# Layer 0's product: six blocks in the first pass over the matrix, with a maximum of their own

## The chip, the cores and the metric

The kernel runs on one core of one Trainium2 chip. The metric is the device time of one execution in microseconds (us); smaller is better. A core has TensorE (PE; it multiplies matrices and writes PSUM, a memory of eight banks of 512 fp32 columns in 128 partitions), VectorE (DVE), ScalarE (ACT), GpSimd (POOL), and SyncE (SP), which here only issues transfers (DMAs). Each engine takes its instructions in order; they wait for one another by semaphores (`wait_ge`, `then_inc`).

## What is computed

A graph network of four layers over N = 2708 nodes with D = 128 features. All share one adjacency matrix `adj` (2708 x 2708 fp32, 29 MB, some nine entries a row, all positive in these inputs). Layers 0 and 1, which the change touches:

```python
# layer 0
hw = x @ W
h_plus, h_minus = (adj > 0) @ hw, (adj < 0) @ hw
e_plus  = leaky_relu(h_plus @ a1 + h_minus @ a2, 0.2)      # one score per node
e_minus = leaky_relu(h_minus @ a1 + h_plus @ a2, 0.2)
scores  = where(adj > 0, e_plus[None, :], where(adj < 0, e_minus[None, :], -9e15))
x = layernorm(x + softmax(scores, axis=1) * adj @ hw)
# layer 1
A = adj + eye;  d = A.sum(1) ** -0.5
x = layernorm(x + relu(d[:, None] * A * d[None, :] @ (x @ W1.T + b1)))
# layers 2 and 3: attention with four heads, then messages with gelu,
# both over the non-zero entries; layernorm after each
```

Without negative entries each column of the softmax is a weight `exp(e_plus[j] - max)`. Layer 0 is then a product of `adj` with hw scaled per node, divided by the sums of the weights over each row's non-zero entries.

## The kernel before

**Tiling.** The 2708 nodes are 22 blocks of 128 rows, the last (block 21) of 20. A block of `adj` or its transpose is 1354 KB. `ring` holds nine blocks of the transpose, `rows` two blocks of `adj` itself. The output columns are six chunks (five of 512, one of 148), one PSUM bank each (banks 0 to 5). SP issues the ring's loads, POOL most of the rows' loads.

**First pass** (0 to 122 us). Every transposed block is loaded (`load_ring`, L841), ScalarE turns it into its signs in bf16 (`binT`, L1019), and TensorE adds `signs x u` for all nodes in 22 products of four columns (L122, `ps<-u,binT`); u = hw @ a1 lies in `u3`. The last block gives the scores (`zd`, L1574), their maximum goes through TensorE to all partitions (`nmx0`, L1587), ScalarE makes the weights (L1025).

**Extraction.** VectorE takes from every block of `adj` the eight largest entries and their places in each of six segments of 452 columns (`extract_segment`, L1532 and L1522), then the rest for that block (`extract_rest`), which also gives the row sum for layer 1 (`dinv`). A block is seven pieces. `FIRST` = 5 blocks are extracted in the first pass, up to `AHEAD` = 15 during layer 0's product, 18 pieces in the transition, the rest after it. POOL loads a rows buffer again when its block is extracted (`v_row`, L962), and does a lookup per block. Later layers need the edges found this way.

**Layer 0's product** (to 212, then in a transition to 303). Blocks go backwards, 21 to 0: the last nine are still in the ring. ScalarE scales hw by the weights (L1032) and makes the signs again (L1039). TensorE does six chunks of the share (`share0`, fp32, `ps<-ring,hwu`) and six of the sums of weights (`weight_sums`, bf16, banks 6 and 7). The last `TAIL` = 7 blocks are done chunk by chunk (`tail0`), so that a finished chunk can be transposed, normalised and projected for layer 1 while the next is computed (the loop over `SLOTS`, L1092 and L1313).

**Layer 1** (303 to 360). Nine blocks, 0 to 8, are in the ring; blocks 0 to 7 are multiplied within the transition (`shares1_until`), block 8 on in a loop, the last `TAIL1` = 5 by chunks (`tail1`). hw1 of blocks below `AHEAD` is scaled by 1/sqrt(row sum) as it is made (`projected1`). For the others `scaled_late` (L1082) does square root and scaling when ScalarE comes to block `LATE` = 14 of its own loop: 22 passes that look for negative entries (L1117). TensorE waits for that at block 15. VectorE waits for the square root in `row_scales`, with nothing of the extraction left behind it. After its loop ScalarE copies finished chunks from PSUM (L1053). VectorE waits for the end of ScalarE's loop (`c_neg`) ahead of `after_layer1`.

**Layers 2 and 3** (to 786) gather rows from tables in HBM with indirect DMAs from POOL (L939). `near0` is such a table; only the path for other inputs reads it.

## Time and profile before

| | |
|---|---|
| median of three runs | 786.44 us (783.33 to 786.92) |
| the profiled execution | 787.66 us |
| its span, first to last instruction | 785.9 us |
| PE busy / DVE / ACT / POOL | 445.2 / 480.0 / 301.0 / 333.8 us |
| DMA moved | 117.20 MB, mean 149 GB/s |
| mean granted TensorE clock | 0.747 |

A row of the view by stages gives the stretch, its length, the busy time of PE, of its weight loads (PEld), DVE, ACT and POOL, each with its count of instructions, the granted clock, the DMA share and GB/s.
### The profile page before, as it was taken

Reading aid. Unit: us, or ns where it says so; the run is one execution under the profiler, and the core shown is the slowest. Engines: PE = TensorE matmul, PEld = TensorE weight load, DVE = VectorE, ACT = ScalarE, POOL = GpSimd, SP = SyncE. Lnnn points to the kernel's source line nnn. Section 1 sums busy time; section 2 is a strip of 40 time slices with the busy share of each in tenths; the row PEclk is TensorE's granted clock in tenths of the full one; section 3 lists DMA queues with packets and bytes.
Section 4 is the critical chain, followed back from the end, with each engine's and each line's share of the span. In section 5 each row is a group of like instructions: output and inputs, shape, how many; then the busy total and the mean of one; then the engine's idle time right before and its main releaser. Section 6 shows DMA issues by size and latency. Waiting matters only on the chain.

```text
span 785.9 us, 6700 instructions
## 1 busy us (share of the span) xinstructions
PE 445.2 (57%) x1987; PEld 269.0 (34%) x1987; DVE 480.0 (61%) x1457; ACT 301.0 (38%) x363; POOL 333.8 (42%) x492
## 2 busy tenths in 40 slices
PE   4221118999999999999843855304504404405231
PEld 4121113444455655444632734203303303303120
DVE  2419608988946569523454559539849749748564
ACT  3565364458823316995611302203213213213131
POOL 7204502555522126400055356726636736736700
PEclk9555555999999999999865886656757757757655
DMA  8999992999712124990022211211112112111200
GB/s 317 367 424 420 398 324 110 365 398 387 298 71 72 56 72 156 425 374 1 28 73 56 73 44 43 54 30 51 47 37 50 52 32 51 50 33 50 54 8 13
DMA packets 32697, 117.20 MB, mean 149 GB/s; under 512 B 8518, under 2 KB 19636, under 8 KB 23892
## 3 DMA queue, kind: packets, MB, share of 16 engines
q1 hardware_dynamic: 19970, 78.21, 25.3%
q0 software_dynamic: 9952, 38.49, 15.5%
q10 hardware_dynamic: 2734, 0.01, 0.2%
q8 instruction: 17, 0.28, 0.1%
q14 instruction: 24, 0.20, 0.1%
HBM read 111.15 MB, written 5.55 MB: 148 GB/s over the span
## 4 chain that ended last, share of the span: by engine, by line
PE 40%; DVE 25%; DMA 11%; issue 10%; another core or an unknown queue 8%; ACT 3%; SPq 1%; ACTq 0%; DVEq 0%
PE ps L122 38%; DMA ring<-in_adjT_dram 11%; DVE agg L1858 4%; DVE G L1855 3%; DVE G L1843 2%; DVE A L1747 1%; DVE st L1761 1%; DVE M L1725 1%; SPq L842 1%; DVE Mh L1724 1%; DVE t L1779 1%; DVE t L1782 1%; DVE t L1781 1%; DVE yo L1788 1%
## 5 line engine op out<-in xcount | busy, mean ns | idle before, releaser
L939 POOL DMA_INDIRECT G<-near,IX x147 | 140.3, 954 | 44.8 <-issue 44.8
L122 PE MATMUL ps<-ident,agg 128*128 128x128 f32 (+1 forms) x44 | 14.3, 420 | 192.6 <-DVE agg L1858 160.2
L122 PE MATMUL ps<-ring,hwu 128*128 128x512 f32 (+3 forms) x264 | 114.3, 586 | 1.0 <-ACT hwu L1032 1.0
L122 PE MATMUL ps<-ring,xT_s 128*128 128x512 f32 (+1 forms) x264 | 108.0, 553 | 0.0
L1522 DVE FIND_INDEX8 I<-V,rows 128x8 uint32<-128x452 f32 (+1 forms) x132 | 82.1, 627 | 0.0
L939 POOL DMA_INDIRECT Go<-near,IO x44 | 43.6, 990 | 89.7 <-DVE IO L1741 59.5
L1532 DVE MAX8 V<-rows 128x8 f32<-128x452 f32 (+1 forms) x132 | 79.9, 618 | 0.8
L122 PEld LDWEIGHTS ps<-ident,agg 128*128 128x128 f32 (+1 forms) x44 | 9.4, 260 | 198.2 <-DVE agg L1858 162.6
L122 PEld LDWEIGHTS ps<-ring,hwu 128*128 128x128 f32 (+1 forms) x264 | 51.0, 203 | 63.9 <-issue 62.7
L1019 ACT ACTIVATE binT<-ring 128x2708 bf16<-128x2708 f32 (+1 forms) x22 | 53.9, 2459 | 45.2 <-DMA ring<-in_adjT_dram 45.2
L1039 ACT ACTIVATE binT<-ring 128x2708 bf16<-128x2708 f32 (+1 forms) x22 | 53.9, 2456 | 29.5 <-PE ps L122 29.5
L962 POOL DMA_DIRECT2D rows<-in_adj_dram x18 | 10.9, 606 | 125.7 <-DVE I L1522 125.7
L122 PE MATMUL ps<-u,binT 128*128 128x4 bf16 (+1 forms) x484 | 18.1, 167 | 80.5 <-ACT binT L1019 80.5
L122 PE MATMUL ps<-E,M 128*128 128x273 f32 (+2 forms) x192 | 53.9, 440 | 16.1 <-DVE IO L1741 8.7
L122 PEld LDWEIGHTS ps<-ring,xT_s 128*128 128x128 f32 x264 | 45.5, 192 | 43.7 <-issue 43.1
L1117 ACT ACTIVATE binT<-ring 128x2708 bf16<-128x2708 f32 (+1 forms) x22 | 53.8, 2444 | 0.0
L939 POOL DMA_INDIRECT G<-near2f,WIX x22 | 21.6, 983 | 75.6 <-DMA near2f<-hwu 69.2
L122 PEld LDWEIGHTS ps<-E,M 128*128 128x128 f32 x192 | 40.2, 232 | 29.2 <-issue 22.1
L122 PEld LDWEIGHTS ps<-u,binT 128*128 128x128 bf16 (+1 forms) x484 | 16.0, 103 | 82.7 <-ACT binT L1019 79.6
L1188 ACT ACTIVATE std<-mv,eps 128x2 f32<-128x2 f32 x22 | 6.5, 296 | 95.6 <-remote 44.2
L969 POOL TENSOR_TENSOR look<-places,posf 128x336 f32<-128x336 f32 (+1 forms) x22 | 16.4, 744 | 56.4 <-DVE posf L1551 56.4
L1858 DVE TENSOR_REDUCE agg<-G 128x128 f32<-128x1024 f32 x21 | 39.5, 1881 | 0.7
(258 smaller groups left out, 843.9 us busy)
## 6 DMA issues: line engine op xcount, KB each, us to landing
ring<-in_adjT_dram SPq DMA_DIRECT2D x46, 1354.0 KB, 15.5
rows<-in_adj_dram POOLq DMA_DIRECT2D x17, 1354.0 KB, 9.5
rows<-in_adj_dram SPq DMA_DIRECT2D x4, 1354.0 KB, 23.7
G<-near,IX POOLq DMA_INDIRECT x147
xT_s<-in_xT_dram SPq DMA_DIRECT2D x1, 1354.0 KB, 6.3
near<-hwu SPq DMA_DIRECT2D x1, 1344.0 KB
out_dram<-yo SPq DMA_DIRECT2D x21, 64.0 KB
near2f<-hwu SPq DMA_DIRECT2D x5, 256.0 KB
```

Of the source, the lines that this page charges most:

```text
L122: return pe.matmul(dst, lhsT, rhs, start=start, stop=stop, skip_group_check=True)
L939: pool.indirect_dma_start(out=dst, out_offset=None, in_=table, in_offset=bass.IndirectOffsetOnAxis(ap=index, axis=0), engine_sem=o_g).then ...
L962: pool.dma_start(rows[0:rn(n + ROWS), n % ROWS, :], adj[(n + ROWS) * P:(n + ROWS) * P + rn(n + ROWS), :]).then_inc(s_later[n % ROWS], 16)
L969: lk.done(pool.tensor_tensor(look[0:r, :, :], places[0:r, :].unsqueeze(1).broadcast_to([r, TOP, SEGS * 8]), posf[0:r, n, :].unsqueeze(2).b ...
L1019: act.activation(binT[0:rn(j), j % 2, :], ring[0:rn(j), j % RING, :], ACT.Sign).then_inc(c_sg, 1)
L1039: act.activation(binT[0:rn(j), p % 2, :], ring[0:rn(j), j % RING, :], ACT.Sign).then_inc(c_sg, 1)
L1117: act.activation(binT[0:rn(j), j % 2, :], ring[0:rn(j), j % RING, :], ACT.Relu, scale=-1.0, accum_out=negs[0:rn(j), j:j + 1]).then_inc(c_n ...
L1522: return dve.max_index(I64[0:rn(n), n % 2, 8 * s:8 * s + 8], V64[0:rn(n), n % 2, 8 * s:8 * s + 8], segment(n, s))
L1532: dve.max(V64[0:rn(n), n % 2, 8 * s:8 * s + 8], segment(n, s)).then_inc(v_max, 1)
L1843: dve.tensor_tensor(G3[0:r, q, 0:TOP, :], G3[0:r, q, 0:TOP, :], own.unsqueeze(1).broadcast_to([r, TOP, D]), ALU.add).then_inc(v_pre, 1)
L1855: few.done(dve.tensor_tensor(at, at, slot_weights[0:r, n, :].unsqueeze(2).broadcast_to([r, TOP + 1, D]), ALU.mult))
L1858: dve.tensor_reduce(agg[0:r, n % 2, :], at.rearrange("p k d -> p d k"), AX.X, ALU.add).then_inc(v_agg, 1)
```

## The change

Six blocks of layer 0's product, 9 to 14 (`TAKEN`), are done in the first pass. Their scores are needed early, so xT is first multiplied by a replicated column `wa_all`, which leaves u of all nodes in every partition of banks 0 to 5, and VectorE computes the six blocks' scores from their rows of `adj` (`zdA`), the maximum of these six, and the weights against that maximum. Four of the six blocks of rows lie in ring slots until they are extracted (`HELD`), two in `rows`; they are loaded first, and extracted first (`EXTRACT`). The transposed blocks are loaded as 9 to 14, 2 to 8, 15 to 21, 0, 1 (`STREAM`); the sixth to ninth of them each wait for an extraction to free a slot, the tenth to fifteenth for a share of TensorE. When the global maximum is known, ScalarE multiplies banks 0 to 5 in place, and VectorE banks 6 and 7, by `fall` = exp(own maximum - global maximum), and 16 blocks follow (`LAYER0`: 15 to 21, 0, 1, 2 to 8). The row sums by signs move to bank 5. near0 is stored after the last load. `AHEAD` is 14, and the late scaling has two batches: extractions 14 to 16 (blocks 8, 15, 16), square root at ScalarE's block 4, needed at TensorE's block 8; and 17 to 21, at 14, needed at 17. The product that folds the attention vector of layer 2 moves from the pass to the transition. The gathers no longer count a semaphore of their issue. The diff, cut to its core:

```diff
-EARLY = 4
-FIRST = 5
-AHEAD = 15
-LATE = 14
+GROUP = 6
+HELD = GROUP - ROWS
+FIRST = 8
+AHEAD = 14
+LATE = [(14, 4), (17, 14)]
...
+        by_rows, maxima, folded = bank(5, 152, 4 * NB), bank(5, 256, P + 4), bank(7, 32, 9)
...
+        TAKEN = list(range(RING, RING + GROUP))
+        AGAIN = list(range(2 * RING + GROUP - NB, RING))
+        KEPT = list(range(RING + GROUP, NB)) + list(range(2 * RING + GROUP - NB))
+        STREAM = TAKEN + AGAIN + KEPT
+        LAYER0 = KEPT + AGAIN
+        REST = len(LAYER0)
...
+        FIRST1 = HELD + NB + len(AGAIN) - RING
+
+        def slot(q):
+            return (q - FIRST1) % RING
+
+        def landed(q):
+
+            return 16 * (q // RING + 1)
...
+        def at_pass(i):
+            return HELD + i
+
+        def at_layer0(p):
+            return HELD + NB - RING + p
+
+        def at_layer1(j):
+            return FIRST1 + j
+
+
+        EXTRACT = TAKEN + [n for n in range(NB) if n not in TAKEN]
...
+        BATCHES = [0, AHEAD] + [first for first, _ in LATE[1:]] + [NB]
...
+            for t in range(GROUP):
+                n = EXTRACT[t]
+                if t < HELD:
+                    load_ring(t, n, adj)
+                else:
+                    sp.dma_start(rows[:, (t - HELD) % ROWS, :], adj[n * P:n * P + P, :]).then_inc(s_rows[(t - HELD) % ROWS], 16)
+            for i in range(NB):
+                past = at_pass(i) - RING
+                if 0 <= past < HELD:
+                    sp.wait_ge(v_row, past + 1)
+                elif past >= HELD:
+                    sp.wait_ge(c_sg, past - HELD + 1)
+                    if past - HELD < GROUP:
+                        sp.wait_ge(p_l0, past - HELD + 1)
+                load_ring(at_pass(i), STREAM[i])
+            sp.wait_ge(c_hw, 8)
...
+            for p in range(len(AGAIN)):
+                sp.wait_ge(p_l0, GROUP + p + 1)
                 sp.wait_ge(c_sg, NB + p + 1)
-                load_ring(NB - RING - 1 - p)
+                load_ring(at_layer0(RING + p), AGAIN[p])
...
-                                        in_offset=bass.IndirectOffsetOnAxis(ap=index, axis=0), engine_sem=o_g).then_inc(signal, 16)
-
-
-            for dst, src in [(w2c[:, 0:D], w2), (w2T_s, w2T), (w1T_s[:, :], w1T), (w3c[:, 0:D], wdT),
+                                        in_offset=bass.IndirectOffsetOnAxis(ap=index, axis=0)).then_inc(signal, 16)
...
+                if HELD <= t < NB - ROWS:
+                    to, b = EXTRACT[t + ROWS], (t - HELD) % ROWS
+                    if t + ROWS == FIRST:
+                        pool.wait_ge(c_sg, NB - 2)
+                    pool.wait_ge(v_row, t + 1)
+                    pool.dma_start(rows[0:rn(to), b, :], adj[to * P:to * P + rn(to), :]).then_inc(s_later[b], 16)
+                pool.wait_ge(v_pos, t + 1)
...
+            for i, j in enumerate(STREAM):
+                if i == 2:
+                    act.wait_ge(v_e, 3)
+                    act.activation(wts[:, 0, TAKEN[0]:TAKEN[0] + GROUP], eeA[:, :], ACT.Exp, bias=nm1[:, 0:1]).then_inc(c_w, 1)
+                    act.wait_ge(c_w, 1)
+                    for k, n in enumerate(TAKEN):
+                        act.activation(hws[:, k, :], hwu[:, n, 0:D], ACT.Copy, scale=wts[:, 0, n:n + 1]).then_inc(c_hws, 1)
+                act.wait_ge(s_ring[slot(at_pass(i))], landed(at_pass(i)))
+                if i >= 2:
+                    act.wait_ge(p_e, i - 1)
+                    if i - 2 < GROUP:
+                        act.wait_ge(p_z, i - 1)
+                act.activation(binT[0:rn(j), i % 2, :], of_ring(at_pass(i), rn(j)), ACT.Sign).then_inc(c_sg, 1)
...
+            act.activation(fall[:, :], nm1[:, :], ACT.Exp, bias=nmx0[:, 0:1], scale=-1.0).then_inc(c_w, 1)
+            act.wait_ge(c_w, 3)
...
+            for at, m in chunks:
+                act.activation(ps[:, at:at + m], ps[:, at:at + m], ACT.Copy, scale=fall[:, 0:1]).then_inc(c_w, 1)
...
+            def scaled_late(k):
+                first, last = BATCHES[k + 1:k + 3]
+                act.wait_ge(v_rs, 2 * k + 3)
+                act.activation(dinv[:, 0, first:last], dinv[:, 0, first:last], ACT.Sqrt, bias=ones[:, 0:1]).then_inc(c_dinv, 1)
+                act.wait_ge(v_rs, 2 * k + 4)
                 act.wait_ge(c_hw1, CH)
-                for n in range(AHEAD, NB):
-                    last = act.activation(hw1[0:rn(n), n, :], hw1[0:rn(n), n, :], ACT.Copy, scale=dinv[0:rn(n), 1, n:n + 1])
-                last.then_inc(c_hw1, 1)
+                for t in range(first, last):
+                    n = EXTRACT[t]
+                    late = act.activation(hw1[0:rn(n), n, :], hw1[0:rn(n), n, :], ACT.Copy, scale=dinv[0:rn(n), 1, t:t + 1])
+                late.then_inc(c_hw1, 1)
...
+                for k, (_, at) in enumerate(LATE):
+                    if j == at:
+                        scaled_late(k)
...
+            for at, m in chunks:
+                last = mm(pe, ps[:, at:at + m], wa_all[:, :], xT_s[:, at:at + m], True, True)
+            last.then_inc(p_hw, 1)
...
+            def share_in_pass(i):
+                for at, m in chunks:
+                    last = mm(pe, ps[:, at:at + m], hws[:, i, :], of_ring(at_pass(i), P)[:, at:at + m],
+                              i == 0 and m == BANK, False)
+                last.then_inc(p_l0, 1)
+
+            for i, j in enumerate(STREAM):
+                pe.wait_ge(c_sg, i + 1)
+                for n in range(NB):
+                    last = mm(pe, by_rows[:, 4 * n:4 * n + 4][0:rn(n), :], binT[0:rn(j), i % 2, n * P:n * P + rn(n)], u3[0:rn(j), j, :],
+                              False, i == NB - 1)
+                last.then_inc(p_e if i < NB - 1 else p_ecol, 1)
+                if i < GROUP:
+                    if i == 0:
+                        pe.wait_ge(v_w3, 1)
+                    sums_of_weights(j, i % 2, i == 0)
+                    pe.wait_ge(c_hws, i + 1)
+                    share_in_pass(i)
...
+                    if p == 0:
+                        pe.wait_ge(c_w, 3 + c + 1)
+                    last = share0(p, c)
...
+                for k in range(len(LATE)):
+                    if j == min(EXTRACT[BATCHES[k + 1]:BATCHES[k + 2]]):
+                        pe.wait_ge(c_hw1, CH + k + 1)
...
+            dve.wait_ge(p_hw, 1)
+            for t in range(GROUP):
+                if t < HELD:
+                    dve.wait_ge(s_ring[slot(t)], landed(t))
+                    at = of_ring(t, P)
+                else:
+                    dve.wait_ge(s_rows[t - HELD], 16)
+                    at = rows[:, t - HELD, :]
+                few.done(dve.scalar_tensor_tensor(out=unused, in0=at, scalar=0.0, in1=ps[:, 0:N], op0=ALU.is_gt, op1=ALU.mult,
+                                                  accum_out=zdA[:, t:t + 1]))
+            few.done(dve.scalar_tensor_tensor(out=eeA[:, :], in0=zdA[:, :], scalar=SLOPE, in1=zdA[:, :], op0=ALU.mult, op1=ALU.max))
+            dve.tensor_reduce(emA[:, :], eeA[:, :], AX.X, ALU.max).then_inc(v_e, 1)
...
+            dve.wait_ge(c_w, 1)
+            weights_in_parts(slice(TAKEN[0], TAKEN[0] + GROUP))
...
+            dve.wait_ge(c_w, 3)
+            for to, b, m in ((slice(0, P), 6, BANK), (slice(0, 32), 7, BANK), (slice(32, 64), 7, chunks[5][1])):
+                dve.tensor_scalar(bank(b, 0, m)[to, :], bank(b, 0, m)[to, :], fall[to, 0:1], None, ALU.mult)
+            weights_in_parts(slice(0, NB))
...
+            done = at0 + 3 * CH
+            for k in range(1, len(BATCHES) - 1):
+                extract(done, BATCHES[k + 1] * BLOCK)
+                done = BATCHES[k + 1] * BLOCK
+                row_sums(k)
+                if k + 1 < len(BATCHES) - 1:
+                    extract(done, done + 2)
+                    done += 2
+                row_scales(k)
```

## Rows read from the trace of the kernel before

**Rows 1.** Stages: busy PE, PEld, DVE, ACT, POOL; clock, DMA share, GB/s

```profile
0.00:116.00 116.00, 27.90 (x513) 24.83 (x513) 47.32 (x183) 57.22 (x31) 39.16 (x94) 0.60 0.99 380
122.50:132.80 10.30, 10.24 (x18) 3.94 (x18) 9.99 (x37) 5.88 (x7) 1.59 (x3) 0.50 0.10 20
132.80:138.40 5.60, 5.60 (x8) 2.46 (x8) 5.60 (x17) 2.75 (x2) 3.73 (x9) 0.50 0.98 412
138.40:212.60 74.20, 74.20 (x288) 33.15 (x287) 65.24 (x235) 50.81 (x35) 42.60 (x88) 1.00 0.95 378
303.00:359.50 56.50, 56.50 (x169) 28.16 (x168) 25.88 (x95) 56.23 (x54) 16.35 (x38) 1.00 0.76 309
```

**Rows 2.** ScalarE, first pass: start, duration, line, operation, count, idle before

```profile
42.01 2.46 ACT L1019 ACTIVATE binT<-ring 128x2708 bf16<-128x2708 f32 x1 [4.04 <-DMA ring<-in_adjT_dram]
45.27 2.46 ACT L1019 ACTIVATE binT<-ring 128x2708 bf16<-128x2708 f32 x1 [0.80 <-DMA ring<-in_adjT_dram]
```

**Rows 3.** Start of one extraction, of the next, and the load freed between

```profile
123.16 0.28 DVE L1531 TENSOR_TENSOR rows<-rows,others 128x128 f32<-128x128 f32 x1
131.54 0.28 DVE L1531 TENSOR_TENSOR rows<-rows,others 128x128 f32<-128x128 f32 x1
130.64 0.60 POOL L962 DMA_DIRECT2D rows<-in_adj_dram  x1 [33.46 <-DVE I L1522]
```

**Rows 4.** End of the pass and start of layer 0, four engines

```profile
117.45 0.82 PE L122 MATMUL ps<-u,binT 20*128 20x4 bf16 x22 [1.52 <-ACT binT L1019]
118.31 0.23 DVE L1574 TENSOR_REDUCE zd<-ps 128x21 f32<-128x63 f32 x1 [26.62 <-PE ps L122]
121.76 0.31 ACT L1025 ACTIVATE wts<-ee,nmx 128x22 f32<-128x22 f32 x1 [4.36 <-DVE nmx L1587]
122.56 9.39 PE L122 MATMUL ps<-ring,hwu 20*128 20x512 f32 x12 [1.03 <-ACT hwu L1032]
```

**Rows 5.** Reads of PSUM by VectorE and ScalarE in the transition

```profile
234.32 1.13 DVE L1638 SCALAR_TENSOR_TENSOR tt<-ps,rz,X 128x128 f32<-128x128 f32 x4
218.93 0.60 ACT L1053 ACTIVATE accT<-ps 128x512 f32<-128x512 f32 x1 [1.42 <-PE ps L122]
```

**Rows 6.** Layer 0 blocks in the chain of waits; then TensorE at its tail

```profile
151.56 5.20 PE ps L122 x17
156.83 5.20 PE ps L122 x17
212.62 2.84 PE L122 MATMUL ps<-ring,hwu 128*128 128x512 f32 x6
```

**Rows 7.** Two microseconds of the first pass, columns as in Rows 1

```profile
18.00:19.00 1.00, 0.18 (x2) 0.06 (x1) 0.44 (x3) 1.00 (x3) 0.00 (x0) 1.00 1.30 201
22.00:23.00 1.00, 0.00 (x0) 0.00 (x0) 0.90 (x3) 1.00 (x1) 0.00 (x0) 0.81 1.28 298
```

**Rows 8.** ScalarE in layer 1, in order of time

```profile
303.13 2.44 ACT L1117 ACTIVATE binT<-ring 128x2708 bf16<-128x2708 f32 x1
337.35 0.28 ACT L1085 ACTIVATE dinv<-dinv,ones 128x7 f32<-128x7 f32 x1
337.90 2.16 ACT L1089 ACTIVATE xT_s<-xT_s,dinv 128x128 f32<-128x128 f32 x7 [0.27 <-DVE dinv L1606]
```

**Rows 9.** VectorE at the end of the extractions, in order of time

```profile
291.17 0.28 DVE L1531 TENSOR_TENSOR rows<-rows,others 128x128 f32<-128x128 f32 x1
324.55 0.17 DVE L1602 TENSOR_TENSOR dinv<-dinv,diag 128x7 f32<-128x7 f32 x1
337.66 0.20 DVE L1606 RECIPROCAL dinv<-dinv 128x7 f32<-128x7 f32 x1 [12.95 <-ACT dinv L1085]
```

**Rows 10.** TensorE in layer 1, in order of time

```profile
314.26 0.38 PE L122 MATMUL ps<-ident,xT_s 128*128 128x128 f32 x2
363.84 0.65 PE L1276 MATMUL ps<-ident,accT 128*128 128x128 f32 x4
```

**Rows 11.** A gather of layer 2 on POOL

```profile
400.83 0.96 POOL L939 DMA_INDIRECT G<-near2f,WIX  x1 [0.30 <-issue]
```

More of the change, by code:

```diff
@@ L839, in _, with load_ring @@
             sp.dma_start(xT_s[:, 0:N], xT).then_inc(s_x, 16)
-            def load_ring(j):
-                sp.dma_start(ring[0:rn(j), j % RING, :], adjT[j * P:j * P + rn(j), :]).then_inc(s_ring[j % RING], 16)
-            def load_rows(n):
-                if n >= ROWS:
-                    sp.wait_ge(v_row, n - ROWS + 1)
-                sp.dma_start(rows[0:rn(n), n % ROWS, :], adj[n * P:n * P + rn(n), :]).then_inc(s_rows[n % ROWS], 16)
-            for j in range(NB):
-                if j >= RING:
-                    sp.wait_ge(c_sg, j - RING + 1)
-                load_ring(j)
-                if j in (1, 4, 9, 13):
-                    load_rows((1, 4, 9, 13).index(j))
-                if j == NB - 8:
-                    sp.wait_ge(c_hw, 8)
-                    sp.dma_start(bass.AP(near0.tensor, 0, [[D, P], [P * D, NB - 1], [1, D]]), hwu[:, 0:NB - 1, 0:D]).then_inc(s_near, 16)
-                    sp.dma_start(near0[P * (NB - 1):N, :], hwu[0:LAST, NB - 1, 0:D]).then_inc(s_near, 16)
+            def load_ring(q, j, of=adjT):
+                sp.dma_start(of_ring(q, rn(j)), of[j * P:j * P + rn(j), :]).then_inc(s_ring[slot(q)], 16)
@@ L1239, in share0, with sums_of_weights @@
-            def share0(j, c):
-                at, m = chunks[c]
-                return mm(pe, ps[:, at:at + m], hwu[0:rn(j), j, 0:D], ring[0:rn(j), j % RING, at:at + m], j == NB - 1, j == 0)
-            def weight_sums(p):
-                j = NB - 1 - p
-                pe.wait_ge(c_sg, NB + p + 1)
+            pe.wait_ge(v_u3, 1)
+            for half in range(2):
+                mm(pe, bank(5, 256 * half, 256), zeros, w3[:, 0:8, :].rearrange("p n w -> p (n w)"), True, False)
+            def sums_of_weights(j, binary, first):
@@ new lines, in _, with share0, weight_sums @@
+            pe.wait_ge(v_e, 4)
+            mm(pe, maxima[0:2, 0:P], emx[:, :], ident[:, :], False, True).then_inc(p_gm, 1)
+            pe.wait_ge(v_e, 6)
+            mm(pe, maxima[:, P + 2:P + 4], ones[0:2, :], gm[0:2, 0:2], False, True).then_inc(p_gm, 1)
+            def share0(p, c):
+                at, m = chunks[c]
+                j = LAYER0[p]
+                return mm(pe, ps[:, at:at + m], hwu[0:rn(j), j, 0:D], of_ring(at_layer0(p), rn(j))[:, at:at + m], False, p == REST - 1)
+            def weight_sums(p):
+                pe.wait_ge(c_sg, NB + p + 1)
+                sums_of_weights(LAYER0[p], p % 2, False)
@@ L1265, in tail0 @@
             def tail0(c):
-                for j in range(TAIL - 1, -1, -1):
+                for p in range(MAIN0, REST):
                     if c == 0:
-                        pe.wait_ge(c_hws, NB - j)
-                        pe.wait_ge(s_ring[j % RING], in_layer0(j))
-                    last = share0(j, c)
+                        q = at_layer0(p)
+                        pe.wait_ge(c_hws, GROUP + p + 1)
+                        pe.wait_ge(s_ring[slot(q)], landed(q))
+                    last = share0(p, c)
                 last.then_inc(p_tail, 1)
@@ L1294, in share1 @@
                 at, m = chunks[c]
[L1295 removed]
+                last = mm(pe, ps[:, at:at + m], hw1[0:rn(j), j, :], of_ring(at_layer1(j), rn(j))[:, at:at + m], j == 0, False)
                 if j // 4 == c:
@@ new lines, in _, with lies, segment, places_of @@
+            dve.wait_ge(c_w, 1)
+            weights_in_parts(slice(TAKEN[0], TAKEN[0] + GROUP))
+            dve.wait_ge(k_set, 16)
+            def lies(t):
+                r = rn(EXTRACT[t])
+                return of_ring(t, r) if t < HELD else rows[0:r, (t - HELD) % ROWS, :]
+            def segment(t, s):
+                return lies(t)[:, s * SEG:min((s + 1) * SEG, N)]
+            def places_of(t, s):
+                r = rn(EXTRACT[t])
+                dve.wait_ge(v_max, t * SEGS + s + 1)
+                return dve.max_index(I64[0:r, t % 2, 8 * s:8 * s + 8], V64[0:r, t % 2, 8 * s:8 * s + 8], segment(t, s))
@@ L1608, in _, with row_scales @@
+            def row_scales(k):
+                b = slice(*BATCHES[k:k + 2])
+                dve.wait_ge(c_dinv, k + 1)
+                dve.reciprocal(dinv[:, 1, b], dinv[:, 0, b]).then_inc(v_rs, 1)
             dve.wait_ge(s_diag, 32)
-            dve.wait_ge(v_pos, AHEAD)
-            row_sums(slice(0, AHEAD))
+            row_sums(0)
             def stats(c):
```

260 lines of the change are left out of this document (116 added, 144 removed).

## The prediction

> **What bounds the kernel now.** I read the profile by stages first, then the order of time on each engine at the seams. [rows 1] show four regimes. Up to 116 us the transfers are the bound: DMA share 0.99 at 380 GB/s, TensorE busy 27.9 of 116 us. From 122.5 to 212.6 TensorE never stops: layer 0's product. The clock is 0.50 until 138.4 (1.2 GHz) and 1.00 (2.4 GHz) after that; before the rise it first worked on the block of 20 rows (122.5 to 132.8) and then 5.6 us on a full block. DMA stands at 0.95 to 0.98 there too, but TensorE waits for nothing. From 303 to 359.5 two engines are full at once, TensorE 56.5 and ScalarE 56.2 of 56.5 us: layer 1's product beside the 22 passes that look for negative entries. After about 397 come layers 2 and 3, which the change hardly touches. So work taken out of 122.5 to 212.6 pays in full, what lengthens the first pass costs in full, and whatever makes ScalarE wait after 303 costs in full as well.
>
> **The gain in layer 0.** The product leaves six of 22 blocks to the first pass. A warm block (six chunks of the share and six of the weights' sums) has a pitch of 5.27 us (151.56 to 156.83, [rows 6]): 6 x 5.27 = 31.6 us less. Also, the first block of the stage is now a full one (block 15), and the 20-row block comes seventh. If the clock rises after 5.6 us instead of 15.8 (122.6 to 138.4, [rows 1]), half the difference is saved: 5.1 us. Against that, the 20-row block now lies in the middle: the engine was idle from about 18 and its clock fell in the microsecond after 22 [rows 7], and that block takes about as long as that idle stretch. The bounds are 0 (clock stays) and 5.6/2 = 2.8 (it falls and has to rise again); no row is nearer to one than to the other, I take 1.4. Stage: -31.6 -5.1 +1.4 = -35.3.
>
> **The cost in the first pass, until the product can start.** What the six blocks need first: six row blocks of adj, loaded ahead of the transposed ones. Transposed block i=1 is then the eighth big load after xT, as block 5 is now: it lands at 42.0 [rows 2]. Loads follow at 3.26 us (42.01 to 45.27). The sixth lands 6.5 us before the eighth, 35.5. VectorE's scores are six passes over 2708 columns out of PSUM, which before doesn't have. A 128-column one takes 1.13/4 = 0.28 us [rows 5]; if all of that scaled with columns it were 6.0 us, if 0.15 of it is fixed, 2.9. I take 3.0, as one extraction segment of 452 columns is part of a block that runs 2708 columns twice in 8.38 us [rows 3]. Last score at 38.5, maximum through TensorE and back as in the later chain (3.45 us, [rows 4]) about 42: ScalarE is then still signing block i=1 (42.0 to 44.5), so even 5 us per score would cost only 2 us. Exp 0.3, the weights in three parts 1.2: the extractions start at 46.1 instead of about 22.
>
> That matters because four ring slots hold adj rows until they are extracted. The first extraction gives its slot back after 7.1 us (DVE 123.16, the wait on POOL's load ended before 130.64), the next ones 8.38 us apart [rows 3]: 53.2, 61.6, 70.0, 78.3. SP issues i=5 to i=8 only then, and everything behind them waits in SP's queue. The five loads before them are through at 51.8. So from 51.8 to 79.5 the DMA engines move three loads instead of eight: a hole of some 17 us. From 78.3 on 13.2 ring loads and two of rows remain: 15.2 x 3.26 = 49.4, with 1.2 us for the first bytes (share 0.10 over 10.3 us after POOL's issue at 130.64, [rows 1, 3]): 128.9. Then POOL, let go by the third last sign at about 125, starts a row load while 2.7 us of ring load are outstanding. Bounds 0 (it takes turns after it) and 3.3 (a whole load ahead of it); both queues run together in the whole of the first pass, so I take 2.7: last landing 131.6. The Trainium skill, DMA: Bandwidth & Descriptors, Queues, rings and completion order, says that each SDMA engine round-robins between the queue rows with work; by that rule it is 2.7, by a strict order it would be 0 and the whole sum better by 2.7. No row here separates the two.
>
> TensorE's new work in the pass: six blocks of about 6 us (5.27 and 0.82 for the row sums, [rows 4, 6]) from 46 on, one stretch of 5.6 us cold: done at about 84. The SP queue needs the sixth for i=14, which the transfers reach only at 78.3 + 1.2 + 8 x 3.26 = 105.6. Hidden. The scores' product from the replicated column (six chunks, about 4.6 us at 8.6 to 13) delays hwu to 23: hidden, it is needed at 42. DVE's 8 extractions end at 113: hidden.
>
> From last landing to product: sign 2.5, row sums 0.86, scores and maximum 3.45, exp to product 0.80 [rows 2, 4]; new: the factor's exp 0.3 and the first in-place rescale, 0.60 as a copy of such a chunk [rows 5]; the other five lie under cold shares of 1.7 us each. 8.5 us: product starts at 140.1 instead of 122.56 [rows 4], +17.5. The near0 table, now stored behind the last load, lands at about 137 and is needed at 139: hidden, up to 3 us if not. VectorE's rescale of banks 6 and 7 (three ops, under 2 us) and the weights lie under the first cold block. The folded weights' product moves from the pass to the transition: +0.6.
>
> Seam of the layers: -35.3 +17.5 +0.6 = -17.2 (tail at 195.4 instead of 212.6, [rows 6]). VectorE has six extractions there, 50.3 us from 142, done at about 194 with waits, needed at 201: hidden.
>
> **What layer 1 takes back.** In times of before (all shifted by -17.2): eight extractions are left after the fourteenth, 2.6 go into the transition. Batch 14 to 16 is ready at 291.2 [rows 9], two pieces more at 293.5; then VectorE waits for the square root that ScalarE does at its block 4. ScalarE starts its passes at 303.13, 2.445 each ((337.35-303.13)/14, [rows 8]): 312.9. VectorE, in order, stands for 20 us with five extractions behind that wait. Before has the same wait, 12.95 us, but with no extraction behind it [rows 9]. TensorE wants block 8 at 311.6 (314.26 less three chunks, [rows 10]) and now needs blocks 8, 15, 16 scaled: sqrt 0.3, reciprocal 0.3, three copies of 0.31 (2.16/7, [rows 8]): 314.5, a stall of 2.9. VectorE goes on at 313.5: 5 x 8.38 - 1.95 = 40.0, done 353.5 instead of 324.55 [rows 9]. ScalarE reached block 14 at 339 and waits 15 us; scales done 356.1, eight passes 19.6: 375.7, first copy of the sums 376.3. TensorE's row transposes of chunk 0 start then instead of at 363.84 [rows 10]: +12.5, and they stood behind it 9.6 us idle, long enough for the clock to fall [rows 7]: +2.8 (0 if it holds). Layer 1 takes back 15.3.
>
> **Sum.** -17.2 + 15.3 = -1.9 us. Layers 2 and 3: the same instructions; the gathers lose one semaphore update. A gather issues every 1.25 us, 0.95 of it busy and 0.30 "issue" [rows 11]. Bounds: nothing, or all of the 0.30; I take 0, since nothing shows that the gap is the update's. The profiled execution took 787.66 (span 785.9): 785.8 expected. It lies 1.2 over the median of the three runs; 786.44 - 1.9 = 784.5.
>
> **Rivals.** (1) TensorE stays cold in the first pass, slower: blocks of 9.4 + 1.0 + 0.8 = 11.2 us end at 112.6, i=14 is issued then instead of by 105.6, eight loads follow (7.2 x 3.26), the last lands at 139.9: +8.3, 792.8. It decides from 9.9 us per block on ((105.6-46.1)/6). For it: 0.50 in all of the pass now. Against: that is with 22 tiny products every 3.3 us; at full blocks the clock rose after 5.6 us [rows 1]. 0.15. (2) Other waits at the new seams (near0, clock twice down, row loads late behind ring loads): +3 to +8, 790. 0.18. (3) Layer 1 gives nothing back, if ScalarE comes to its block 4 before VectorE stands: 784.5 - 15.3 = 769. Against: the order of instructions leaves no way; for: I may have a wait's turn wrong. 0.12. (4) The gap between gathers was the update: 22 gathers of layer 2 and the first 18 of layer 3 are waited for, 40 x 0.30 = 12: 772.5 or less. 0.08. (5) The hole is filled better than I count (loads of POOL, faster scores), half of 17: 776. 0.05. The sum as it stands, 780 to 789: 0.42. That the change doesn't compute in the pass at all would be a variant of (1): 31.6 back, no more than 816; no chance of its own.
>
> **Chances and range.** Over 0.5% (3.9 us) is what a measurement here can tell. Faster: 0.12 + 0.08 + 0.05 and 0.10 of the sum's own spread: 0.35. Slower: 0.15 + 0.10 of (2) + 0.06: 0.31. Same: 0.34. Since both signs hold most of it: the likeliest case alone is 780 to 789; the range that leaves 2 in 10 outside is 770 to 795.
>
> **What would show it.** First pass: DMA tenths low between 52 and 79 us, sixth share done near 84, product at 140. Layer 0: tail from 195, PEclk 5 for only one slice's third after 140, perhaps a dip at the seventh block. Layer 1: VectorE idle 20 us for the square root, ScalarE 15 us at its block 14, TensorE about 10 us ahead of the first row transposes, each 17 us earlier than quoted. Wrong if the hole isn't there, if extractions end before 340, or if gathers come every 0.95 us.

## The result and the profile after

The changed kernel takes 790.12 us (median of 14 executions, 786.95 to 793.39), the kernel before 784.88 (782.06 to 786.92): ratio 1.006, 95% interval 1.0042 to 1.0077, 4.7 us slower. Measured again beside three experiments it was 1.0068 (1.0048 to 1.0088). Forecast was 784.5, 1.9 us under before; the time lies in the range, the sign is wrong. The profiled execution took 789.33 (span 787.6), 1.7 over that of before (787.66): it is this difference that the trace can explain, and "What stays open" below says what is left of the rest.

Four marks cut both traces into stages: the first matmul of the product, the last projection of layer 0, the first row transposes of layer 1's sums and the first gather of layer 2. All times are us.

| | before | changed | stage's difference | forecast |
|---|---|---|---|---|
| product starts | 122.56 | 143.91 | +21.4 | +17.5 |
| last projection | 302.05 | 288.13 | -35.3 | -34.7 |
| first row transposes, layer 1 | 363.84 | 364.50 | +14.6 | +12.5 |
| first gather, layer 2 | 399.12 | 401.92 | +2.1 | +2.8 |
| end of the span | 785.9 | 787.6 | -1.1 | 0 |
| sum | | | +1.7 | -1.9 |

So the product did give what was expected, and 21 us went into the first pass and 15 into layer 1. The view by stages (columns as in [rows 1]) of the changed kernel:

```profile
52.00:80.00 28.00, 28.00 (x196) 14.09 (x193) 27.45 (x100) 12.30 (x5) 16.30 (x33) 1.00 0.51 178
80.00:116.00 36.00, 8.93 (x224) 7.58 (x222) 31.26 (x115) 19.76 (x9) 13.17 (x30) 0.55 1.01 425
116.00:143.90 27.90, 6.12 (x136) 4.96 (x137) 3.93 (x14) 16.04 (x11) 10.63 (x22) 0.50 1.05 363
143.90:148.30 4.40, 4.39 (x6) 1.83 (x7) 4.20 (x15) 4.40 (x8) 0.00 (x0) 0.50 0.37 92
148.30:182.70 34.40, 34.40 (x135) 15.23 (x134) 32.08 (x118) 28.93 (x23) 17.99 (x36) 1.00 0.89 352
182.70:189.10 6.40, 6.40 (x20) 2.61 (x19) 6.26 (x24) 3.88 (x3) 3.81 (x10) 0.50 0.90 352
```

First row: the six blocks' shares fill TensorE at full clock while DMA stands at 0.51 and 178 GB/s: this is the hole in the loads that the prediction counted. Second row: from 80 on the transfers are again the only bound. Fourth and sixth: the clock rises 4.4 us into the product, where it took 15.8 before, but falls once more for 6.4 us in the middle, with TensorE busy all the time.

The end of the pass, in order of time on each engine (start, duration, idle time ahead and what ended it), answers to [rows 4]. A row of ACTq or SPq is the issue of a transfer by that engine and the time it took; the transfer itself goes on after it:

```profile
104.95 29.10 SPq L897 DMA_DIRECT2D near<-hwu  x1
131.27 2.46 ACT L1058 ACTIVATE binT<-ring 128x2708 bf16<-128x2708 f32 x1 [0.75 <-DMA ring<-in_adjT_dram]
131.74 10.12 ACTq L1061 DMA_DIRECT2D diag<-in_adj_dram  x1
138.87 0.15 DVE L1696 TENSOR_SCALAR nmx<-ps 128x1 f32<-128x1 f32 x1
142.28 0.31 ACT L1065 ACTIVATE wts<-ee,nmx 128x22 f32<-128x22 f32 x1 [8.56 <-issue]
143.91 2.90 PE L123 MATMUL ps<-ring,hwu 128*128 128x512 f32 x3 [5.15 <-ACT ps L1084]
```

The maximum is in all partitions at 138.9, yet the exponential starts at 142.28: its idle time ends with "issue", not with VectorE as in [rows 4]. The instruction ahead of it in ScalarE's list, the second transfer of the diagonal, takes 10.12 us to issue. Before, the same one took 3.95 and was over ahead of the maximum:

```profile
114.52 3.95 ACTq L1022 DMA_DIRECT2D diag<-in_adj_dram  x1
```

Both kernels issue the diagonal in two transfers. The first, of 10.5 KB, took 0.43 us in each; the second holds only the 20 elements of the last block (0.1 KB), and it is this one that took 3.95 and 10.12. SP shows the same (first row above): its second store of near0, 10 KB, held SP for 29.10 us.

Layer 1 answers to [rows 8 to 10]:

```profile
299.30 0.18 DVE L1715 RECIPROCAL dinv<-dinv 128x3 f32<-128x3 f32 x1 [17.41 <-ACT dinv L1129]
300.64 3.38 PE L123 MATMUL ps<-ring,xT_s 128*128 128x512 f32 x5 [2.72 <-ACT xT_s L1134]
342.11 0.16 DVE L1709 TENSOR_TENSOR dinv<-dinv,diag 128x5 f32<-128x5 f32 x1
342.31 0.30 ACT L1129 ACTIVATE dinv<-dinv,ones 128x5 f32<-128x5 f32 x1 [17.39 <-DVE dinv L1709]
363.88 1.05 ACT L1096 ACTIVATE moved<-ps 128x512 f32<-128x512 f32 x2
364.50 1.12 PE L1348 MATMUL ps<-ident,moved 128*128 128x128 f32 x4 [9.59 <-ACT moved L1096]
365.41 7.00 PE L123 MATMUL ps<-ring,xT_s 128*128 128x512 f32 x10
```

A chain of three waits: VectorE stands 17.4 us for a square root that ScalarE does at its block 4; its last five extractions are late by that; ScalarE stands 17.4 us for them at its block 14; TensorE stands 9.6 us for ScalarE's copy of the sums. Ten matmul records behind that take 7.00 us, most of it at half clock (the same ten take 4.65 at 1.00, from 373.28 in this trace).

The gathers are as before, 0.95 us busy and 0.30 "issue" each (44.8/147), so the removed count cost nothing [rows 11]:

```profile
L972 POOL DMA_INDIRECT G<-near,IX x147 | 140.3, 954 | 44.8 <-issue 44.8
```

### The profile page after: what moved, and what is told of

The parts are those of the page before. It is cut to its first block, busy times and chain, and to the rows that moved or that the text cites. A ratio compares the mean times of both kernels' runs of the same rounds, so it can differ in the third digit from the quotient of the medians.

```text
span 787.6 us, 6760 instructions
## 1 busy us (share of the span) xinstructions
PE 448.7 (57%) x2004; PEld 268.2 (34%) x2004; DVE 504.5 (64%) x1487; ACT 289.6 (37%) x367; POOL 332.9 (42%) x490
## 4 chain that ended last, share of the span: by engine, by line
PE 33%; DVE 25%; DMA 12%; issue 12%; another core or an unknown queue 9%; ACT 6%; ACTq 1%; SPq 1%; DVEq 0%
PE ps L123 31%; DMA ring<-in_adjT_dram 11%; DVE agg L1977 4%; DVE G L1974 2%; DVE G L1962 2%; DVE I L1636 2%; DMA rows<-in_adj_dram 2%; DVE V L1645 1%; ACT binT L1164 1%; ACTq L1061 1%; DVE A L1866 1%; DVE M L1844 1%; ACT binT L1058 1%; DVE st L1880 1%
## 5 line engine op out<-in xcount | busy, mean ns | idle before, releaser
L972 POOL DMA_INDIRECT G<-near,IX x147 | 140.3, 954 | 44.8 <-issue 44.8
L123 PE MATMUL ps<-ring,xT_s 128*128 128x512 f32 (+2 forms) x336 | 141.7, 567 | 2.7 <-ACT xT_s L1134 2.7
L123 PE MATMUL ps<-ring,hwu 128*128 128x512 f32 (+2 forms) x192 | 82.6, 584 | 5.2 <-ACT ps L1084 5.2
L123 PEld LDWEIGHTS ps<-ring,xT_s 128*128 128x128 f32 (+1 forms) x336 | 60.3, 197 | 66.4 <-issue 63.3
L1058 ACT ACTIVATE binT<-ring 128x2708 bf16<-128x2708 f32 (+1 forms) x22 | 53.9, 2458 | 55.7 <-DMA ring<-in_adjT_dram 36.5
L1636 DVE FIND_INDEX8 I<-V,rows 128x8 uint32<-128x452 f32 (+1 forms) x108 | 66.7, 621 | 0.0
L1645 DVE MAX8 V<-rows 128x8 f32<-128x452 f32 (+1 forms) x108 | 64.9, 614 | 0.6
L1164 ACT ACTIVATE binT<-ring 128x2708 bf16<-128x2708 f32 (+1 forms) x22 | 53.7, 2443 | 0.0
L123 PEld LDWEIGHTS ps<-ring,hwu 128*128 128x128 f32 (+1 forms) x192 | 36.8, 202 | 49.3 <-issue 43.0
L1080 ACT ACTIVATE binT<-ring 128x2708 bf16<-128x2708 f32 (+1 forms) x16 | 39.2, 2457 | 9.7 <-PE ps L123 9.7
L1866 DVE TENSOR_SCALAR A<-iota,erow,entry 128x256 f32<-128x256 f32 x44 | 15.4, 411 | 40.1 <-remote 39.8
```

Of the source, the lines that this page charges most:

```text
L123: return pe.matmul(dst, lhsT, rhs, start=start, stop=stop, skip_group_check=True)
L972: pool.indirect_dma_start(out=dst, out_offset=None, in_=table, in_offset=bass.IndirectOffsetOnAxis(ap=index, axis=0)).then_inc(signal, 16)
L1058: act.activation(binT[0:rn(j), i % 2, :], of_ring(at_pass(i), rn(j)), ACT.Sign).then_inc(c_sg, 1)
L1080: act.activation(binT[0:rn(j), p % 2, :], of_ring(q, rn(j)), ACT.Sign).then_inc(c_sg, 1)
L1164: act.activation(binT[0:rn(j), j % 2, :], of_ring(q, rn(j)), ACT.Relu, scale=-1.0, accum_out=negs[0:rn(j), j:j + 1]).then_inc(c_neg, 1)
L1636: return dve.max_index(I64[0:r, t % 2, 8 * s:8 * s + 8], V64[0:r, t % 2, 8 * s:8 * s + 8], segment(t, s))
```

## The experiments

Distances are from the kernel before on the same chip, worked out from the ratio and its 95% interval times before's median there (784.6 to 786.4 us, except where noted). The changed kernel stands at +4.7 and +5.3: +5.0 below. Each such distance has an interval of 1.4 to 2.3 us to either side, so a difference of two is good to some 2 us; the times in the traces say more where they are given.

**The diagonal's transfers.**

```diff
 # end of ScalarE's first pass
-act.dma_start(diag[:, 0:NB - 1], ...)
-act.dma_start(diag[0:LAST, NB - 1:NB], ...)
 # SP, behind the loads of X
+sp.dma_start(diag[:, 0:NB - 1], ...)
+sp.dma_start(diag[0:LAST, NB - 1:NB], ...)
```

> The two transfers of the diagonal go from ScalarE's queue, where the exponential of the weights stands behind their issue (10.12 us from 131.74, the exponential at 142.28), to SP's, behind the loads of X. Theory: the maximum is known at 138.9, so the exponential starts 3.4 us earlier, the product at 140.5 instead of 143.91, and the kernel is 3 to 4 us faster than the changed one (ratio to it 0.996). Rival: the wait for near0's store or VectorE's work on the sums ends just as late, or layer 1 takes the gain back because VectorE's extractions set its end: less than 1 us.

Measured: ratio 1.0017 (0.9996 to 1.0038), +1.3 us: 3.7 faster than the changed kernel. The exponential and the second transfer now, in order of time:

```profile
139.44 0.31 ACT L1065 ACTIVATE wts<-ee,nmx 128x22 f32<-128x22 f32 x1 [5.27 <-DVE nmx L1696]
143.76 3.40 SPq L902 DMA_DIRECT2D diag<-in_adj_dram  x1
```

The releaser is VectorE's maximum again, the product starts at 141.06 instead of 143.91, layer 1's first row transposes come at 362.47 instead of 364.50, and the first gather at 398.60 instead of 401.92. The theory holds; the rival (near0, or layer 1 taking it all back) doesn't. Issued at 143.76, behind the other loads, the transfer takes 3.40 us.

**The two late square roots**, one at a time and together:

```diff
-LATE = [(14, 4), (17, 14)]
+LATE = [(14, 0), (17, 14)]     # first move
+LATE = [(14, 4), (17, 18)]     # second move
+LATE = [(14, 0), (17, 18)]     # both
```

> The first of layer 1's two late square roots is asked for ahead of ScalarE's block 0 instead of block 4. VectorE stood 17.41 us for it (until 299.30) although its sums were ready at 281.9. Theory: it goes on at about 290, the extractions end at 332.8 instead of 342.11, ScalarE's wait at block 14 falls from 17.39 to about 8, TensorE's stall of 2.72 at block 8 and its idle time of 9.59 ahead of the transposes of layer 1's end go, and with the latter the half clock behind it (2.3): 11 to 13 us faster than the changed kernel. Rival: extractions are bound by the loads of rows, which the ring's loads hold up, and the gain is under 5 us.

> The second late square root is asked for ahead of ScalarE's block 18 instead of 14, so that four passes (2.44 us each) run while VectorE still extracts. Theory: ScalarE's passes end 9.8 us earlier (354.1 instead of 363.88), TensorE's idle 9.59 becomes under 1, and the clock doesn't fall: 10 to 12 us faster than the changed kernel. Rival: TensorE then waits as long for the last five blocks' scaled rows, whose copies come behind the same square root at 342.1: under 3 us.

> Both moves at once. Theory: they remove the same wait of ScalarE (one from each side), so the gains don't add: TensorE alone bounds layer 1, 14 to 15 us faster than the changed kernel, 2 to 3 more than either alone, which makes about 775.5, some 9 us faster than the kernel before. Rival, that layer 1 took back nothing that order in ScalarE's list can return (TensorE's own work at the lower clock instead): within 3 us of the changed kernel.

Measured: 0.9925 (0.9902 to 0.9948), 0.9936 (0.9914 to 0.9957), 0.9928 (0.9903 to 0.9953): -5.9, -5.0 and -5.7 us, so 10.9, 10.0 and 10.7 faster than the changed kernel. Each alone turns the loss into a gain. With the first move VectorE waits 9.3 us and ScalarE 7.3:

```profile
291.22 0.17 DVE L1715 RECIPROCAL dinv<-dinv 128x3 f32<-128x3 f32 x1 [9.34 <-ACT dinv L1129]
334.28 0.30 ACT L1129 ACTIVATE dinv<-dinv,ones 128x5 f32<-128x5 f32 x1 [7.29 <-DVE dinv L1709]
```

With both, ScalarE waits for no extraction any more, and TensorE for no copy of the sums:

```profile
290.68 0.18 DVE L1715 RECIPROCAL dinv<-dinv 128x3 f32<-128x3 f32 x1 [9.35 <-ACT dinv L1129]
306.18 2.84 PE L123 MATMUL ps<-ring,xT_s 128*128 128x512 f32 x6 [1.79 <-DMA ring<-in_adjT_dram]
317.08 2.84 PE L123 MATMUL ps<-ring,xT_s 128*128 128x512 f32 x6 [1.11 <-DMA ring<-in_adjT_dram]
340.54 0.28 ACT L1129 ACTIVATE dinv<-dinv,ones 128x5 f32<-128x5 f32 x1
349.32 6.86 PE L123 MATMUL ps<-ring,xT_s 128*128 128x512 f32 x14 [0.79 <-DMA ring<-in_adjT_dram]
356.11 0.66 PE L1348 MATMUL ps<-ident,moved 128*128 128x128 f32 x4
```

The wait and its cause are shown: the gains don't add, because both remove the same wait. I expected 11 to 13 from the first move and 10 to 12 from the second, which came within 0.1, but 14 to 15 for both and got 10.7. From last projection to row transposes it takes 66.3 us (289.82 to 356.11), before 61.8: TensorE now waits 3.7 us for ring loads, which it did nowhere in this stage before. That rows of `adj` are still loaded there beside them, because extractions are left, is the likely reason; no run separated it.

**A control on the kernel before**: its one late square root at 18 instead of 14 (`LATE = 18`).

> A control: the kernel before, with its one late square root ahead of ScalarE's block 18 instead of 14. Theory: there TensorE waits for nothing between 300 and 370 and ScalarE reached block 14 just as the extractions were done (337.35 against 337.66), so layer 1 has nothing to return: within 1.5 us of before. Rival: the move of the square root is worth some 10 us to any version, and the gain of the second experiment has nothing to do with the change: 5 us or more faster.

This kernel, and those below with the short block first, with four blocks, and with the queue and both square roots together, ran on a chip where before takes 708.67 us: there layers 2 and 3 are some 77 us shorter, the stages ahead the same within some 2 us (the last section). Ratio 1.008 (1.0055 to 1.0106), +5.7 us: slower. The rival is out, since the move brings before nothing; but the theory's "within 1.5 us" missed too. I had overlooked that before's one batch begins with block 15, so a square root ahead of ScalarE's block 18 is late for TensorE. (The expectation also misread [rows 9]: the sums were ready at 324.55, 12.8 us before ScalarE came to block 14; 337.66 is the reciprocal behind its square root.)

```profile
347.60 5.32 PE L122 MATMUL ps<-ring,xT_s 128*128 128x512 f32 x8 [3.57 <-ACT xT_s L1089]
```

Before, TensorE waits for nothing between 300 and 370; the wait that the moves remove is thus one that the change made. As the control is slower for a reason of its own, it shows this only from one side.

**The short block first.** To test what pulled the clock down at 182.7:

```diff
-KEPT = list(range(RING + GROUP, NB)) + list(range(2 * RING + GROUP - NB))
+KEPT = [NB - 1] + list(range(RING + GROUP, NB - 1)) + list(range(2 * RING + GROUP - NB))
```

> The block of 20 rows leads the product (and the last nine of the first pass) instead of standing between blocks 20 and 0. Theory of the clock: the granted clock stays at half a few us longer at the product's start, but the fall to 0.50 from 182.7 to 189.1, which came right behind the 12 products of 20 rows (6.58 us), doesn't happen: 3 us faster than the changed kernel, product's clock 1.00 from its rise to 230. Rival 1: the fall has another cause (the loads, the wait behind the rescaling) and comes at the same time: no change. Rival 2: the short block now stretches the cold start by as much: 0 to 1 us slower.

Measured: 1.0087 (1.0063 to 1.011), +6.2 us: 1 us slower than the changed kernel, which is rival 2. Stages of its product:

```profile
145.20:161.00 15.80, 15.80 (x25) 6.37 (x26) 15.56 (x54) 11.06 (x13) 5.45 (x12) 0.50 0.50 184
161.00:200.00 39.00, 39.00 (x161) 17.77 (x161) 34.91 (x130) 31.84 (x22) 23.26 (x47) 1.00 0.94 363
```

The fall in the middle is gone, so far the theory (a shorter one, at 210 to 220, stays; the changed kernel has it too). But the clock rises only 15.8 us after the start, as long as in [rows 1], where this block is first too. The cost at the start, 11.4 us more at half clock (5.7 us of time), is larger than the 3.2 that the fall saved. Its profiled execution was the slowest of six, 3.4 us over their median, so the later times of that trace say less. My "3 us faster" counted the second effect and left out the first, though the prediction itself had read it from [rows 1].

**Full rows for the short block**, in its old place:

```diff
-hwu[0:rn(j), j, 0:D], of_ring(at_layer0(p), rn(j))[:, at:at + m]
+hwu[0:P, j, 0:D], of_ring(at_layer0(p), P)[:, at:at + m]
```

> The product's six matmuls of the block of 20 rows take 128 partitions: rows 20 to 127 of its projections are zero, and its slot holds an older block's numbers there, so the result is the same and the matmuls as long as before. The block stays at its place. Theory: the fall to half clock at 182.7 (6.4 us) was the answer to matmuls that use 20 of 128 rows, so it doesn't come: 3 us faster than the changed kernel. Rival: not the rows but the time or place of the block matters (loads, or the product's length): it falls as before, within 1 us.

Measured: 1.0034 (1.0014 to 1.0054), +2.7 us, and 1.0068 (1.0048 to 1.0088) for the changed kernel beside it: 2.7 faster. The intervals touch, but the traces agree: from the product's start to the last projection 141.9 us (145.14 to 287.08) against 144.6 (144.43 to 289.06). The twelve records of the block in the changed kernel's second run (the fall came between 183 and 186 there) and then, in this one, those of the same block and of the next:

```profile
180.47 6.17 PE L123 MATMUL ps<-ring,hwu 20*128 20x512 f32 x12
```

```profile
180.08 4.81 PE L123 MATMUL ps<-ring,hwu 128*128 128x512 f32 x12
185.79 4.81 PE L123 MATMUL ps<-ring,hwu 128*128 128x512 f32 x12
```

And the granted clock, in the same order of kernels; the numbers are length, busy PE, clock, DMA share, GB/s:

```profile
183.00:186.00 3.00, 3.00 (x6) 0.63 1.00 419
186.00:189.00 3.00, 3.00 (x16) 0.50 0.86 314
```

```profile
183.00:186.00 3.00, 3.00 (x19) 1.00 1.03 437
186.00:189.00 3.00, 3.00 (x8) 1.00 1.00 415
```

Same columns, same place, only 128 rows in place of 20: no fall. That settles the cause of this fall, against the rival.

**Fewer blocks in the pass** (`GROUP = 4`, then `GROUP = 5`).

> Four blocks instead of six take part during the first pass; the last two are left to the product. Theory: the pass is bound by slots that its own extractions free late; with two passes of scores fewer (2 x 3.3) and two slots fewer held, the maximum is known about 10 us earlier (129 instead of 138.9), and the product, two blocks longer (2 x 5.27 = 10.5), ends within 2 us of where it did: what the last two blocks give is what they cost. Extractions begin earlier by 6.6, so layer 1 ends 4 to 6 us earlier: 3 to 7 us faster than the changed kernel. Rival: a taken block costs the pass nothing, the hole in the loads (51.8 to 79.5) stays: the product starts where it did and ends 10.5 later, 5 to 10 us slower.

> Five blocks in the first pass. With four the last sign of the pass began at 115.81, with six at 131.27: 7.7 us for each of the two, against the 5.27 that one takes off the product. Theory: the price is even (each block more is one slot held longer, one pass of scores and one more load held back): last sign at 123.5, layer 0 ends 2.4 us earlier than with six, layer 1's end with it, 2 to 3 us faster than the changed kernel. Rival: the hole opens only with the sixth block (the slots just suffice for five): last sign by 117, 5 us or more faster than the changed kernel, and faster than four.

Measured: four blocks 0.9966 (0.9944 to 0.9988), -2.4 us on its chip, 7.4 faster than six; five blocks 1.0066 (1.0044 to 1.0089), no different from six. Times of the three:

| blocks taken | last sign | issue of the diagonal | exponential | product | last projection |
|---|---|---|---|---|---|
| 4 | 115.81 | 11.87 | 126.46 | 128.23 | 283.44 |
| 5 | 123.41 | 14.98 | 139.24 | 140.87 | 289.39 |
| 6 | 131.27 | 10.12 | 142.28 | 143.91 | 288.13 |

```profile
114.48 11.87 ACTq L1061 DMA_DIRECT2D diag<-in_adj_dram  x1
```

```profile
123.84 14.98 ACTq L1061 DMA_DIRECT2D diag<-in_adj_dram  x1
139.24 0.31 ACT L1065 ACTIVATE wts<-ee,nmx 128x22 f32<-128x22 f32 x1 [13.39 <-issue]
```

The last sign moves by 7.6 and 7.9 us a block: the even price of the theory, against 5.27 saved. The hole doesn't open only with the sixth block. With four blocks the product starts 15.7 us earlier than with six, not the 10 expected, and its last projection comes 4.7 earlier, not within 2. Five blocks were to be 2 to 3 us faster. By the traces the longer issue of the diagonal ate that: the maximum is known at 130.26, the exponential comes 9.0 us later; with six blocks it comes 3.4 later (138.87 to 142.28). So of the 7.9 us between five and six only 3.0 reach the product's start; no run with five blocks and the other queue was made.

**Together.** First the queue and both square roots, then also four blocks and full rows.

> The diagonal's transfers on SP's queue and both late square roots moved (ahead of ScalarE's blocks 0 and 18). Theory: the two remedies act in different stages with TensorE the bound of both, so the gains add: 11.4 + 2.6 = 14 us faster than the changed kernel, 776, about 10 us (ratio 0.987) under the kernel before. Rival: with the product 3 us earlier VectorE's extractions, which don't move as far, set layer 1's end again: 11 to 12 us.

> All at once: four blocks in the first pass, the diagonal's transfers on SP's queue, both late square roots moved, full rows for the short block. Theory: the remedies lie in different stages and TensorE bounds each, so they add: product's start at 125, last projection at 277 (288.8 with the change: -5.3 for four blocks, -3 for the queue, -3 for the clock), layer 1 in the 66.3 us that it took with both square roots moved (289.8 to 356.1), so its first transposes at 343.5 instead of 364.5: 20 us faster than the changed kernel, 15 (ratio 0.978) under the kernel before. Rival: VectorE's extractions become the bound of layer 1, and the gain on the changed kernel stays at the 14 us of the two remedies alone.

Measured: 0.9863 (0.9831 to 0.9895), -9.7 us; and 0.9775 (0.9751 to 0.98), 766.56 us beside 784.62 before and 790.34 changed: -17.7 us, 23 faster than the changed kernel. Both as expected or better (14 and 20 were forecast against the changed kernel, 14.7 and 23 came), so the remedies add. Stages of the last (columns as in [rows 1]):

```profile
0.00:124.40 124.40, 55.31 (x624) 35.35 (x625) 88.49 (x303) 61.37 (x41) 55.19 (x127) 0.70 0.98 381
124.40:274.50 150.10, 149.84 (x556) 76.83 (x556) 95.44 (x370) 76.11 (x105) 47.85 (x99) 0.99 0.45 174
274.50:340.50 66.00, 62.01 (x180) 29.90 (x178) 45.56 (x161) 58.41 (x57) 25.23 (x53) 1.00 0.75 302
340.50:380.00 39.50, 28.73 (x144) 17.99 (x144) 20.93 (x89) 18.66 (x46) 3.24 (x3) 0.96 0.13 39
```

In the first pass DMA has a share of 0.98 again, the product starts 2 us after before's with four blocks done, and TensorE is busy for 212 of the 216 us up to layer 1's end.

## Why the prediction was wrong, step by step

**What bounds the kernel**: right. Time taken from the product came back in full, time added to the pass and to ScalarE's layer 1 cost in full.

**The gain in layer 0**: right in sum, -35.3 against -34.7 with the folded product. The clock rose after 4.4 us instead of the 5.6 taken. The short block's term was outside its bounds: 6.4 us at half clock cost 3.2 (2.7 by the run with full rows), where I took 1.4 and 2.8 at most, half of the 5.6 us of [rows 1]. I took the fall for a case of an idle engine; the run with full rows shows that it belongs to the 20 rows.

**The first pass**: extractions from 44.00 (46.1), the sixth share over at 81.0 (84), the hole (DMA 0.51 from 52 to 80), last sign at 131.27 (131.6). The mechanism is right; that the last number agrees to 0.3 us is luck in part. The slots came free 2 us earlier (the loads' issues at 59.59, 67.96 and 76.34), but the loads landed 5.6 to 6.3 us after their issue, not 4.5. And the 2.7 us for POOL's row load weren't paid. It was issued at 128.47, not at about 125:

```profile
128.47 0.60 POOL L996 DMA_DIRECT2D rows<-in_adj_dram  x1 [28.60 <-ACT binT L1058]
```

From 128 to 132 POOL's queue moved no packet, and the last ring load had landed at 131.24. About as much was lost elsewhere: the last 3.2 loads took 12.1 us (signs at 119.17 and 131.27), not 10.4, and from 120 to 124 DMA moved 295 GB/s at a share of 1.05, beside 423 from 96 to 120. The load of the block of 20 rows lies in that stretch and is the likely reason; no run separated it. The Trainium skill, DMA: Bandwidth & Descriptors, Queues, rings and completion order, has each engine go round-robin between the queue rows that it has work for. The trace agrees for the row load issued at 85.00: from 89 to 95 POOL's queue had 52.1% of the engines' time and SP's 48.5%. No run here shows the case that the term was for. (Two sums in the prediction are slightly off: 15.2 x 3.26 is 49.6, not 49.4, and rival (1)'s six blocks of 11.2 us end at 113.3, not 112.6. The first moves the forecast by 0.2, the second only that rival.)

**The step that failed: "From last landing to product", 8.5 us.** It took 12.6 (131.27 to 143.91). The sum listed what computes, and left out ScalarE's two transfers between the last sign and the exponential. They stand there in the kernel before too, where the issue was over 3.3 us ahead of the exponential and cost nothing; so the wait was put at nothing without looking at what the transfers would meet, now that near0's store and a load of rows run beside them. It held the exponential back by 3.4 us (138.87 to 142.28). With the transfers on SP's queue the step took 9.3 (131.72 to 141.06), 3.3 less, and the kernel was 3.7 faster. The other 0.8 is spread over the rest of the step. That near0's store and the load of rows are what makes the issue longer wasn't tested.

**Layer 1: the mechanism right, the size short.** All three waits came as foretold: VectorE 17.4 (20), TensorE 2.7 (2.9), ScalarE 17.4 (15), TensorE's idle time 9.6 (9.6) and the half clock behind it, 2.35 on ten records and 2.1 on the stage (2.8). The stage took back 14.6 and not 12.5; the term that was small is VectorE's end of the extractions: 336.3 in the forecast's times, 339.6 with the layer shifted by 13.9 instead of 17.2, 342.11 measured, 2.4 of it waits for rows still on their way, which I had as a rival and not in the sum.

**Sum.** +3.9 (pass), -0.6, +2.1, -0.7, -1.1 make the 3.6 between -1.9 and +1.7. **Rivals**: (2), "other waits at the new seams", 790, is the case that came, by two of its three parts (row loads late, the clock down twice; near0 never waited for in the changed kernel, 2.0 us in the one with the short block first), and by one that it doesn't name, the largest. That its 790 is the measured median is luck: the traces account for 3.6 of the 6.6 us between forecast and measured difference. (1) is out by the clock of 1.00 from 52 to 80, (3) by the three waits, (4) by the gathers' unchanged 0.30, (5) by the hole.

**What stays open.** Medians differ by 5 us, the spans of the two profiled executions by 1.7. Of before there is one profile, 2.8 over its median of 14, and the changed kernel's is 0.8 under its own. Up to the first gather the difference is 2.8 us, in the changed kernel's second profile 4.0 (403.07); behind it the same program took 385.7 and 382.1, before 386.8. That spread, with VectorE's waits for gathered rows in it, is as large as what is missing; whether 1 to 2 us of the loss lie in layers 2 and 3 wasn't settled.

## What to carry to other kernels

When work is moved ahead, read the list of the engine that stands at the new seam line by line, transfers included: an issue that was free because its engine had nothing to do becomes a term of the sum. A batch of late work that is asked for at a fixed place in another engine's list has to be placed anew whenever the stages shift: here moving one of two numbers gave 10 to 11 us. And price each block of such a move by itself; with buffers held longer the last two of six cost 7.7 us each and saved 5.3.

## What the runs showed of the hardware

- TensorE, busy all the time, was granted half clock during and behind matmuls that used 20 of 128 rows, in three places: the fall in the middle (6.4 us), and a rise after 15.8 us instead of 4.4 where that block leads, in the kernel before and in the reordered one. With zeros in the other 108 rows the clock stayed at 1.00, for the same number of columns. These are not the only falls of a busy TensorE: in the changed kernel the clock was also at 0.50 from about 210 to 213, behind 2.5 us of products of four columns (from 206.06), and before at 245 to 247 and 282 to 285, each behind some 3 us in which projections of 128 columns alternate with products of a single row. No run separated these.
- The issue of a small transfer can take long on its engine's queue, and in these kernels it is the second of a pair that does. The diagonal's second transfer (20 elements, 0.1 KB, behind one of 10.5 KB that took 0.43 us) took 3.95 us in the kernel before, 3.40 to 6.88 on SP behind the loads of X (three runs), 10.12 in the changed kernel, where the rest of near0's 1344 KB store and two 1354 KB loads of rows ran beside it, and 8.83 to 14.98 in the other eight runs with it at that place. The engine's later instructions waited for its end.
- One chip ran layers 2 and 3 in 308 us (407.84 to 716.2) instead of 386, with gathers of the same pitch (0.95 us busy, 0.30 between). VectorE's waits there for landed rows ("remote") are gone; the group that shows it, from the changed kernel and then from the kernel with the short block first:

```profile
L1866 DVE TENSOR_SCALAR A<-iota,erow,entry 128x256 f32<-128x256 f32 x44 | 15.4, 411 | 40.1 <-remote 39.8
```

```profile
L1866 DVE TENSOR_SCALAR A<-iota,erow,entry 128x256 f32<-128x256 f32 x44 | 15.7, 416 | 0.0
```

Why it is so wasn't looked into; kernels are compared only with the kernel before on the same chip for this reason.
